# Gates in halves over six slots, a projection spread over two slots, and two sets of DMAs on another queue, in a two-layer attention and expert kernel on one core

## The reference, cut to what matters

```python
x = L0_attn_x                                    # (4, 512, 128)
xn = _layernorm(x)
x = x + _L0_attn_ref(xn, ...) + _L0_ffn_ref(xn, ...)
xn = _layernorm(x)
x = x + _L1_attn_ref(xn, ...) + _L1_ffn_ref(xn, ...)

def _L0_ffn_ref(x, w_gate, w_up, w_down):        # HIDDEN = 384, int32 weights / 127
    gate, up = einsum('bsd,hd->bsh', x, wg), einsum('bsd,hd->bsh', x, wu)
    return einsum('bsh,dh->bsd', silu(gate) * up, wd)
```

## Time and profile before

| | |
|---|---|
| median of 3 runs | 544.76 us (542.74 to 545.1) |
| the profiled execution | 544.03 us |
| its span | 542.0 us, TensorE's granted clock 0.95 |
| busy | PE 454.8 us (84%), DVE 400.5 (74%), ACT 328.8 (61%), POOL 262.5 (48%) |
| DMA | 48.27 MB, 89 GB/s on average |

### The profile page before, as it was taken

How to read it: one execution, slowest core, us unless ns; L and a number is a source line. 1 busy time by engine, 2 the same in 40 slices (tenths; PEclk the granted TensorE clock), 3 DMA queues, 4 the chain that set the end, 5 groups by cost and what they waited for, 6 DMA issues and landing times.

```text
span 542.0 us, 9302 instructions
## 1 busy us (share of the span) xinstructions
PE 454.8 (84%) x3394; PEld 169.4 (31%) x3394; DVE 400.5 (74%) x538; ACT 328.8 (61%) x422; POOL 262.5 (48%) x499
## 2 busy tenths in 40 slices
PE   3456979889988999899989898987899999999952
PEld 1101213224322433242312431221245453455511
DVE  5699778886998699869887798789876777623204
ACT  2102666776677667656676577777766567667560
POOL 6861263724425562886378657884201233163240
PEclk9755889999999999999999999999999999999995
DMA  3896596244511360626252645174731111010018
GB/s 82 238 230 89 89 343 106 93 163 146 90 43 61 118 62 4 66 72 127 25 52 39 157 43 56 41 160 68 109 52 32 45 50 50 4 44 25 21 47 219
DMA packets 143742, 48.27 MB, mean 89 GB/s; under 512 B 109890, under 2 KB 139090, under 8 KB 142866
## 3 DMA queue, kind: packets, MB, share of 16 engines
q1 hardware_dynamic: 141394, 42.93, 38.1%
q0 software_dynamic: 2304, 4.76, 2.6%
HBM read 22.81 MB, written 23.14 MB: 85 GB/s over the span
## 4 chain that ended last, share of the span: by engine, by line
PE 53%; DVE 18%; issue 10%; ACT 10%; DMA 4%; SPq 4%; POOL 1%; POOLq 0%; ACTq 0%; DVEq 0%
PE ps L763 14%; DVE mx L1114 11%; PE ps L747 9%; PE ps L732 7%; ACT PT L962 6%; PE ps L802 3%; PE ps L810 3%; PE ps L785 2%; PE ps L803 2%; SPq L433 2%; PE ps L693 2%; PE ps L825 2%; PE ps L822 2%; PE ps L786 1%; DVE th L1135 1%
## 5 line engine op out<-in xcount | busy, mean ns | idle before, releaser
L1114 DVE TENSOR_REDUCE mx<-ps 128x2 f32<-128x1024 f32 x256 | 309.4, 1223 | 73.1 <-PE ps L732 65.1
L962 ACT ACTIVATE PT<-ps 128x1024 f32<-128x1024 f32 x256 | 258.6, 1026 | 125.9 <-PE ps L747 116.5
L763 PE MATMUL ps<-PT,Vp 128*32 128x512 f32 x1024 | 138.1, 611 | 5.4 <-ACT PT L962 4.4
L732 PE MATMUL ps<-KO,QO 48*128 48x512 bf16 (+1 forms) x512 | 104.5, 406 | 39.7 <-ACT PT L962 22.6
L747 PE MATMUL ps<-QO,KO 59*128 59x512 bf16 x512 | 100.2, 390 | 3.8 <-DMA QO<-mT 2.5
L520 POOL DMA_INDIRECT y_tokens<-expert_io,meta x40 | 38.6, 964 | 71.5 <-ACT expert_io L994 48.5
L747 PEld LDWEIGHTS ps<-QO,KO 59*128 59x128 bf16 x512 | 24.6, 93 | 142.8 <-issue 87.9
L1135 DVE SCALAR_TENSOR_TENSOR th<-th,ps 128x320 f32<-128x320 f32 (+1 forms) x44 | 23.8, 541 | 35.2 <-ACT th L978 29.4
L732 PEld LDWEIGHTS ps<-KO,QO 48*128 48x128 bf16 (+1 forms) x512 | 25.6, 96 | 70.9 <-ACT PT L962 38.6
L545 POOL CAST mp<-mx 128x32 bf16<-128x32 f32 x16 | 3.4, 214 | 82.9 <-DVE mx L1114 78.7
L509 POOL DMA_INDIRECT x_places<-xe,place_i x32 | 31.9, 995 | 22.3 <-ACT PT L962 15.2
(11 more groups left out here) (166 smaller groups left out, 475.1 us busy)
## 6 DMA issues: line engine op xcount, KB each, us to landing
z<-part SPq DMA_DIRECT2D x16, 384.0 KB
z<-part SPq DMA_DIRECT2D x16, 256.0 KB
QO<-z SPq DMA_DIRECT2D x64, 48.0 KB
KO<-z SPq DMA_DIRECT2D x64, 48.0 KB
x_places<-expert_io SPq DMA_DIRECT2D x2, 1300.0 KB, 7.4
expert_io<-x_places SPq DMA_DIRECT2D x8, 320.0 KB, 3.5
QO<-z SPq DMA_DIRECT2D x6, 384.0 KB
KO<-z SPq DMA_DIRECT2D x6, 384.0 KB
```

Source lines behind the costliest of these rows:

```text
L732: mm = pe.matmul(ps[:, 2 * pair + half, :], rows_of(QO[u % 3], half, 2 * s + jj, rows, (qt, qt + 1)), rows_of(KO[u % 3], half, 2 * s + jj, ...
L763: last = pe.matmul(ps[32 * g:32 * g + 32, PV_BANK, :], Vp[u % 2][:, k, head(s, g), :], PT[:, (2 * t + g % 2) % 4, g // 2, :], start=(s % 2 ...
L962: act.activation(PT[:, e % 4], ps[:, 2 * pair:2 * pair + 2, :], ACT.Exp).then_inc(exp_done, 1)
L1114: dve.tensor_reduce(mx[:, a, qt, col:col + 5:4], ps[:, 2 * pair:2 * pair + 2, :], AX_X, ALU.max, negate=True).then_inc(max_read, 1)
```

## The change

Four edits are made together.

1. The gates of layer 0 are cut in two by tokens. `G0` = 6 gates a unit of 256 tokens each (`N_TOK0`), one in each of slots 10 to 15, and none in slot 9.
2. Where the unit before belongs to layer 0 (`spread`, units 1 to 4), the projection's four tiles go one by one: tile 0 ahead of the second score of slot 6, tile 1 at the end of slot 6, tile 2 ahead of the second score of slot 7, tile 3 at its end. The residual then goes to slot 8, the rank products to slot 9 (behind the reading of v), their copy to slot 10, and the statistics behind the second reduction of slot 8.
3. The 17 loads of the second layer are issued by ScalarE, after its last qk copy and ahead of the first `maxima_copy`.
4. `empty_places` is issued by ScalarE in slot 9 of units 0 and 1, between that slot's second exponential and the next slot's first.

```diff
         def gate_at(u, slot):
-            return HB * u + slot - 9 if u < B and 9 <= slot < 9 + HB else None
+            return G0 * u + slot - GATE_SLOT if u < B and slot >= GATE_SLOT else None
...
+        G0, N_TOK0, GATE_SLOT = 2 * HB, S // 2, SLOTS_U - 2 * HB
+        def spread(u):
+            return u >= 1 and layer(u - 1) == 0
+        def rank_slot(u):
+            return 9 if spread(u) else 7
...
         def gate_up_0(pe, g):
-            pe.matmul(ps[:, 2 * pair, :], wg[:, cols], xnT[u % 4][:], start=True, stop=True).then_inc(gate_ps[0], 1)
-            pe.matmul(ps[:, 2 * pair + 1, :], wu[:, cols], xnT[u % 4][:], start=True, stop=True).then_inc(up_ps[0], 1)
+            cols, x_T = slice(i * P, (i + 1) * P), xnT[u % 4][:, c * N_TOK0:(c + 1) * N_TOK0]
+            pe.matmul(ps[:, 2 * pair, 0:N_TOK0], wg[:, cols], x_T, start=True, stop=True).then_inc(gate_ps[0], 1)
+            pe.matmul(ps[:, 2 * pair + 1, 0:N_TOK0], wu[:, cols], x_T, start=True, stop=True).then_inc(up_ps[0], 1)
...
             if slot == 6 and u >= 1:
-                out_mms(pe, w, (2, 3))
-            if slot == 7 and p < U and layer(p) == 1:
+                out_mms(pe, w, (1,) if spread(u) else (2, 3))
+            if slot == 7 and spread(u):
+                out_mms(pe, w, (3,))
+            if slot == rank_slot(u) and p < U and layer(p) == 1:
                 pe.wait_ge(unit_done, u)
+                if slot > 8:
+                    pe.wait_ge(v_read, n + 1)
                 rank_mms(pe, p)
...
-                    out_mms(pe, u - 1, (0, 1))
+                    out_mms(pe, u - 1, (0,) if spread(u) else (0, 1))
+                if slot == 7 and spread(u):
+                    out_mms(pe, u - 1, (2,))
                 score_mms(pe, u, slot, 1)
...
                 exponential(act, 2 * t + 1)
+                if slot == 9 and u < 2:
+                    empty_places(act, u)
...
-                if slot == 7 and u >= 1:
+                if slot == (8 if spread(u) else 7) and u >= 1:
                     residual(dve, w)
...
+                if slot == 8 and f < U and spread(u):
+                    statistics(dve, f)
...
-            for dst, src in loads:
-                sp.dma_start(dst, src).then_inc(loaded, 16)
...
+            for dst, src in loads:
+                act.dma_start(dst, src).then_inc(loaded, 16)
             maxima_copy(act, 0, 0)
```

More of the change, by code:

```diff
@@ L336, in across @@
             return ps[:, 2 * pair:2 * pair + 2, :].rearrange("p k n -> p (k n)")[:, a:z]
-        def empty_places(sp, part):
-            sp.wait_ge(empty_ready, part + 1)
-            if part == 0:
-                for k in range(2):
-                    sp.dma_start(y_tokens[k * T:(k + 1) * T].rearrange("(p m n) d -> p m (n d)", p=P, n=8),
-                                 fill_zero.unsqueeze(1).to_broadcast([P, T // P // 8, 8 * D])).then_inc(emptied, 16)
-            first = part * (E // 2) * PLACES
-            sp.dma_start(x_places[first:first + E // 2 * PLACES].rearrange("(e p j) d -> p e (j d)", p=P, j=JE),
-                         fill.rearrange("p (e n) -> p e n", e=E // 2)).then_inc(emptied, 16)
         N_EMPTIED = 16 * 4
@@ L818, in out_mms @@
                 if L == 0:
-                    pe.wait_ge(h_ready[0], HB * (u + 1))
+                    pe.wait_ge(h_ready[0], G0 * (u + 1))
             for t in tiles:
@@ L876, in side_mms @@
                 pe.wait_ge(unit_done, u)
-                if p < U and layer(p) == 1:
+                if p < U and layer(p) == 1 and rank_slot(u) < slot:
                     pe.wait_ge(rank_read, seq(p) + 1)
@@ L883, in side_mms @@
                     pe.wait_ge(v_read, n + 1)
+                if p < U and layer(p) == 1:
+                    pe.wait_ge(rank_read, seq(p) + 1)
                 out_transposes(pe, u, 0)
@@ L970, in half_tanh @@
         def half_tanh(act, L, g):
-            n = S if L == 0 else HALF
+            n = N_TOK0 if L == 0 else HALF
             act.wait_ge(gate_ps[L], g + 1)
@@ L1017, in ranks_copy, with empty_places @@
             act.copy(ranks[:].rearrange("p i t k -> p (i t k)"), ps[:, SIDE, 0:4 * NT * E]).then_inc(rank_read, 1)
+        def empty_places(act, part):
+            act.wait_ge(empty_ready, part + 1)
+            if part == 0:
+                for k in range(2):
+                    act.dma_start(y_tokens[k * T:(k + 1) * T].rearrange("(p m n) d -> p m (n d)", p=P, n=8),
+                                 fill_zero.unsqueeze(1).to_broadcast([P, T // P // 8, 8 * D])).then_inc(emptied, 16)
+            first = part * (E // 2) * PLACES
+            act.dma_start(x_places[first:first + E // 2 * PLACES].rearrange("(e p j) d -> p e (j d)", p=P, j=JE),
+                         fill.rearrange("p (e n) -> p e n", e=E // 2)).then_inc(emptied, 16)
         def scalar_unit(act, u):
@@ L1037, in scalar_unit @@
                     maxima_copy(act, n, 0)
-                if slot == 8 and p < U and layer(p) == 1:
+                if slot == rank_slot(u) + 1 and p < U and layer(p) == 1:
                     ranks_copy(act, p)
                 exponential(act, 2 * t + 1)
+                if slot == 9 and u < 2:
+                    empty_places(act, u)
                 if slot == 0 and u >= 1:
@@ L1131, in gated @@
         def gated(dve, L, g):
-            n, bank = S if L == 0 else HALF, 2 * pair_of(f"gate{L}", g)
+            n, bank = N_TOK0 if L == 0 else HALF, 2 * pair_of(f"gate{L}", g)
             t = th[:, g % 2, 0:n]
@@ L1139, in gated @@
             if L == 0:
-                if g % HB == 0 and g > 0:
-                    dve.wait_ge(y_ps, g // HB)
-                dst = h0_T[:, g % HB, :]
+                if g % G0 == 0 and g > 0:
+                    dve.wait_ge(y_ps, g // G0)
+                dst = h0_T[:, g % G0 // 2, g % 2 * N_TOK0:(g % 2 + 1) * N_TOK0]
             else:
@@ L1191, in vector_unit @@
                     normalize_out(dve, w, 1)
-                if slot == 7 and u >= 1:
+                if slot == (8 if spread(u) else 7) and u >= 1:
                     residual(dve, w)
-                if slot == 8 and f < U:
+                if slot == 8 and f < U and not spread(u):
                     statistics(dve, f)
```

7 lines of the change are left out of this document (2 added, 5 removed).

## The result

| | before | changed |
|---|---|---|
| median | 543.98 us (8 runs, 542.21 to 545.1) | 547.92 us (8 runs, 544.41 to 551.08) |
| ratio | | 1.0078, 95% interval 1.0045 to 1.0111 |
| profiled execution | 544.03, span 542.0 | 547.89, span 545.9 |
| busy PE, DVE, ACT | 454.8, 400.5, 328.8 us | 457.5, 403.4, 330.1 us |

The changed kernel is 0.8% slower, where I had forecast 542.4 with a range up to 547.5. In this text a slot lasts from its first exponential to that of the next slot, and a unit starts with its first exponential. Unit 0 starts at 61.86 us instead of 50.60. Of these 11.26 us, 7.27 are left at the start of unit 1, 4.69 at unit 4, 3.16 at unit 5 and 3.88 at unit 7. So most of the late start was won back later, and 4 us of it were not.

A forecast was written before the change was run, and what follows sets the result against it. No engine bounds it throughout; TensorE, VectorE and ScalarE hand three PSUM pairs round. +2.0 - 3.4 + 2.8 - 2.4 - 1.0 = -2.0 from 544.03 gave 542.0, with the median's offset 542.4; range 538 to 547.5.

The forecast's parts named there:

- start, part 1: Before unit 0's first score: loads moved early to ScalarE overfill the DMA engines; +2.0 us, between 0 and +5.
- hole, part 1: Unit 0, slot 8: the scores' wait for the maxima's rows goes and the clock stays up; -3.4 us, -1.9 to -4.0.
- clearing, part 2: Slot 9 of units 0 and 1: clearing DMAs on ScalarE delay the next exponential; +2.8 us, +1.9 to +4.3.
- gates, part 3: Slots 10 to 15: halved gates shorten gate slots and start the next unit earlier; -2.4 us for four units, -15 to +4.8.
- projection, part 4: Units 1 to 4, slots 6 to 9: tiles spread one by one into idle time; -1.0 us, -2.8 to +1.5.
- the spill: Start: load work not fitting before 46 us, 6.2 us, ends at 52.2 instead of 46; first score 3.0 late.
- The slack: Start: GpSimd's 4.22 us of idling after dequantizing the feed-forward weights, which could absorb their later arrival.
- The upper bound: Start: +5 us, if the whole spill counts or the feed-forward weights come later by more than GpSimd's 4.22 us.
- The rival with the start and the issues at their upper ends: Start at +5 and ScalarE's clearing issues at +4.3 us; median 547; chance 0.12.
- both waits: Spread projection: v products wait some 0.45 us in slot 8, rank products 0.85 in slot 9 for v to be read.
- slots 6 to 8 shorter by 0.24 us: Spread projection, units 1 to 4: following slots 6 to 8, slot 9 begins 0.24 us earlier.
- the second wait: Slot 9: rank products wait 0.85 us for v to be read, while the next maximum matmul waits for an exponential anyway.

The follow-up runs named there:

- e2: The kernel before with only the second layer's 17 loads moved to ScalarE, after its last qk copy; ratio 1.0113.
- e1: The changed kernel with the 17 loads issued by SP again, the other edits kept; ratio 0.9989 against the kernel before.
- b1: The kernel before with halved gates and only the fourteen small loads issued early by ScalarE; 534.65 us beside 539.37, ratio 0.9921.
- e3: The kernel before with only the fourteen small loads issued early by ScalarE, the three large ones left on SP; 536.0 us beside 539.24.
- b3: The kernel before with halved gates, all 17 loads later on SP behind unit 2's operand reads, and the spread projection; 535.46 us, ratio 0.9926.
- b2_again: The kernel before with halved gates and all 17 loads later on SP, no spread projection, timed again; 534.02 us, ratio 0.9898.
- e4: The kernel before with only the three large loads issued early by ScalarE, the fourteen small ones left on SP; 545.57 us beside 539.24.
- e7b: The kernel before with only the spread projection, run again for a further profile; 542.62 us beside 539.37.
- e6: The kernel before with only the gates in halves, both DMA edits and the spread projection undone; ratio 0.9926.
- b2: The kernel before with halved gates and all 17 loads on SP, issued in unit 0 behind unit 2's operand reads; 533.59 us, ratio 0.9904.
- e8: The kernel before with only the clearing moved to ScalarE; ratio 1.0004.
- e0: The kernel before, unchanged, profiled again on the slower chip; run 544.68 us, span 542.3 us.
- e5: The kernel before with all 17 loads on ScalarE, behind a wait for the feed-forward weights; 545.21 us beside 544.25.
- e7: The kernel before with only the spread projection, gates whole and both DMA edits undone; ratio 1.0046.

## Why the prediction was wrong

| term | forecast, us | measured, us | from |
|---|---|---|---|
| start, part 1 | +2.0 (0 to +5) | +10.0 (11.26, less 1.25 in slots 0 to 2) | changed kernel; e2: +7.5 |
| hole, part 1 | -3.4 | -3.4 | slots 7 and 8 of unit 0 |
| clearing, part 2 | +2.8 | +1.25; alone +0.7, in e1 +0.2 | slots 9 and 10 of unit 0 |
| gates, part 3 | -2.4 | -2.8 in slots 9 to 15 and the next slot 0; +0.5 to 1.2 in unit 5 | b1 against e3 |
| projection, part 4 | -1.0 | +1.1 by slots, +1.4 by medians | b3 against b2_again |

**The step that failed is the start.** This is shown by e1 (the start comes back with the loads), e2 and e4 (the large loads alone make it). Its size moves by 2.3 us between profiles: unit 0 starts at 61.86, 59.53 (e2) and 61.09 (e4). I saw that the DMA engines had only 1.8 us free before 46 and that 6.2 us would spill over, but I added the spill at the end of the work, behind everything ("the engines are through at 52.2"), and charged the first score with a part of it. The loads were not behind: they were issued from 20 to 31, ahead of or beside the feed-forward weights (27.6 to 30.6), and shared the engines with them. wd landed 14.8 us after its issue instead of 3.5. The slack that I had named for this, GpSimd's 4.22 us, was used up, and the rest went into the copy of mT: 11.3 later less 4.2 is 7.1, and 6.7 was seen. The upper bound named this path but priced it as an alternative to the spill. The two follow each other, since the backlog that makes wd late also makes SP's issues late, and so puts the 8 KB packets of unit 1's reads ahead of the maxima's rows: 6.7 + 4.6 = 11.3. The bound had to be the sum. From 24 to 34 us packets of both queues are in flight, SP's for 0.56 and ScalarE's for 0.46 of the engines' time: the loads that nobody waits for take it from those that somebody does. The Trainium skill, which the prediction weighed (DMA: Bandwidth & Descriptors, Issuing engines are not separate DMA queues), says that transfers of different engines run on the same 16 DMA engines and interleave. The trace agrees.

The rival with the start and the issues at their upper ends gave 547, near the measured 547.9, but by luck: it had 9.3 for these two where 11.25 were measured, and the difference is made up by slots that no part had in it (below).

**The hole** closed as worked out, with the clock up behind it. Kernels that have it take 9.08 to 9.76 us for slots 7 and 8 (11.26 in e7b, 7.53 in e6), those without 6.37, so -3.4 is the upper end of -2.7 to -3.4. And e3, b1 and b2 show that to move the small loads alone, or to give all a later place on SP, closes it as well.

**The clearing** was put too high. The timeline I followed from an idle queue had 1.9 us for calm issues in front of an exponential, and e1, which has just this order, pays 0.2: slot 9 is 1.1 longer and slot 10 is 0.9 shorter. Alone (e8) they displace idle time before a tanh. In the change a third issue of 1.67 us makes it 1.25.

**The gates** were right in mechanism and nearly in size: slots 10 to 15 of unit 1 take 4.31, 3.57, 4.11, 3.46, 3.14 and 3.47 us for 4.35, 3.5, 4.3, 3.4, 3.2 and 3.7 forecast, and per unit it is -1.1, -0.6, -0.6 and -0.4 for -0.9 and three times -0.5. The forecast had no term for the longer slot 9 of unit 5.

**The projection** had both waits right, 0.47 and 0.84 us in unit 2 for 0.45 and 0.85 forecast. The step that failed is slot 8. I had slots 6 to 8 shorter by 0.24 us in all. Slots 6 and 7 are shorter by 0.23, but slot 8 is longer by 0.38 (0.4 in units 3 and 4, 0.14 in unit 1), so slot 9 begins 0.15 later. That the second wait costs nothing held for units 2 and 3, where slots 9 and 10 pay 0.04 and 0.02. In unit 4, where no gates follow, they pay 0.38.

**The sum.** 10.0 - 3.4 + 1.25 - 2.8 + 1.1 = +6.1, against +3.9 in the two profiled executions. By slots, the difference is made up as follows: slots 3 to 5 of units 3 and 4 take 8.60 and 8.51 us for 9.48 and 9.41 (-1.8); the w_v products of slot 8 in units 3 and 4 take 1.67 each for 2.21 and 2.44 (-1.3); slots 8 and 9 of unit 5 are longer by 0.6; 0.2 are the difference of slot 9 in unit 0 between e3 and before. The first two were in no term of the forecast, and they are not the machine's alone. On the slower kind of chip the short slots go with the halved gates (changed and e6, against before, e0, e5 and e7), and the short w_v products with the spread projection (changed and e7, against before, e0, e5 and e6). On the faster chips they are as short, or nearly so, in all kernels. What lengthens them is open.

## What to carry to other kernels

A load that is moved earlier "into idle time" must be placed among the transfers in flight, not behind them: list what is issued in the same stretch, what waits for each, and its slack, and add the delays along the path that ends last instead of taking the larger one. A share near 1.0 and the bytes per second that go with it don't measure room: from 34 to 46 us 213 GB/s stood at a share of 1.02 before, and 351 at 1.03 after. Before another queue is chosen for a group of DMAs, cut the group. Here the fourteen small loads could go early without harm, the bytes of the three large ones hurt at both places, and a later place for all on the same queue did as well as cutting. Last, compare slots within one kind of chip: slots 3 to 5 of unit 4, which no edit touches, changed by 0.9 us with the kernel on the slower kind and not at all on the others.
